# One core, attention then 64 experts: the first block's routing spread over eight pairs, and the attention's last stages placed between expert tiles

## The chip, the cores and the metric

The kernel runs on one core of a Trainium2 chip. The metric is the device time of one execution in microseconds, the median of several runs. A core has TensorE (PE in the profile; its weight loads are PEld), VectorE (DVE), ScalarE (ACT), GpSimd (POOL) and SyncE (SP, which here only issues DMAs). The engines run their own instruction streams in order and wait for each other on semaphores.

## The reference, cut to what matters

```python
x = x + attn(layernorm(x))      # x: 8 x 512 x 128, 16 heads of 64, biases; attn adds its own
                                # input and ends in a layernorm with gamma and beta
h = layernorm(x)                # 4096 tokens, 128 wide
scores = sigmoid(h @ router_w.T)            # 64 experts in 8 groups
sfc = scores + e_bias                       # choose 4 groups by the sum of their two best,
topk_idx = top8(where(group_chosen, sfc, 0))   # then 8 experts
coef = 2.5 * scores[topk_idx] / sum(scores[topk_idx])      # 0 for the other experts
g, u = h @ Wg[e], h @ Wu[e]                 # every expert, 128 -> 64
moe = sum_e (silu(g) * u * coef[:, e]) @ Wd[e]
out = x + moe + silu(h @ SWg) * (h @ SWu) @ SWd     # and a shared expert 128 -> 128
```

All experts are computed for all tokens, with coefficient 0 where an expert was not chosen. So routing is not sparse work but a chain of small operations that must be ready before a block's experts can be scaled.

## The kernel before

**Attention.** The work is 64 pairs of heads: 8 batches of 512 tokens, 8 pairs each. Each matrix factor is split into a high and a low fp16 part, and a product is three matmuls. Pair p is spread over several steps, each cut into four slots s = 0 to 3. In step p, slot by slot, TensorE computes the transposed scores of pair p (4 matmuls of 512 columns a slot, `ps_st`), the context of pair p-1 (24 short matmuls a slot, bank `ps_ctx`), the row maxima's scores for pairs p+1 and p+2 (2 matmuls a slot, `ps_max2`), in slots 0 and 1 the query and key projection of pair p+3 (`ps_proj`), in slot 2 the value projection of pair p (`ps_proj`), in slot 0 four transposes of the context of pair p-2 and in slot 3 its output product (both `ps_turn`). VectorE takes the row maxima (line 882, `row_max`), low parts (lines 908, 913, 919), the division by the softmax sum (lines 900, 902) and in slot 0 adds the output of pair p-3 to `xn` (line 891). ScalarE takes the exponentials (line 572) and high parts. GpSimd makes the low parts of the exponentials, `lo(s)` at line 437, one for each slot, and the low and high parts of one expert tile's weights over two steps (lines 449 and 453, `split_weights`). TensorE's context in step p+1 waits in slot 0 for all four `lo` of pair p.

`steps` runs p = -3 to 3 written out, p = 4 to 59 in a hardware loop of eight steps (TensorE is written out throughout), and p = 60 to 66 written out. Steps 64, 65 and 66 hold only what is left of pairs 61 to 63: the drain.

**Experts.** Then come 8 blocks of 512 tokens, each of 33 tiles: tile 0 is the shared expert, the others two experts each. A tile is gate and up (3 matmuls each), from tile 1 on one matmul that spreads the coefficients over the hidden rows (`spread`, the selector matrix that `selectors` makes on GpSimd at line 480), and down (3 matmuls). ScalarE applies silu and makes the high part of the hidden values, VectorE multiplies twice (lines 937 and 943), GpSimd makes the low part (line 471). TensorE runs four tiles ahead of `down`.

**Routing.** `route(m, r, k)` is the work of block m in numbered pieces k, the same on all engines: 1 adds the attention's bias, 2 to 6 are the post-norm (ending in line 780, `x2`), 7 to 9 the pre-norm (line 787), 8 on TensorE the transposes to `bank_c(m)`, 11 and 12 their high and low parts, then the logits, the sigmoid (14), the choice of groups (16 to 22) and experts (23 to 26), the coefficients (27, 28), their transposes (27 on TensorE), and their high and low parts (30 and 31). GpSimd has pieces 1 (constants), 2 (beta), 3 and 8 (the power -1/2, line 419) and 14. For blocks 1 to 7, piece k of block m+1 follows tile k of block m. For block 0 the pieces are placed by `block_0_at(p, s)`: pieces 1 to 16 one a slot in steps 60 to 63, and 17 to 31 three a slot from step 64. TensorE's pieces come two later (`route(0, 0, k - 2)`), and its first one waits for the last row maximum. On GpSimd a step's pieces stand behind all its `lo` and the weights. SyncE issues `load_x(0, 0)`, the input of block 0, after all its attention steps. TensorE does `gate_up(0, 0, 0)` in step 65, and the other tiles after step 66 once `spread_done` and, for tile 1, `coef_lo` are there.

The memory of the expert stage lies over buffers that the attention has finished with, in SBUF and in the eight PSUM banks.

## Time and profile before

| | |
|---|---|
| median of 3 runs | 1451.2 us (1448.94 to 1451.33) |
| the profiled execution: its own time | 1443.07 us |
| its span, first to last instruction | 1441.3 us |
| mean granted TensorE clock | 0.990 |
| TensorE matmul busy | 1362.3 us, 95% |
| VectorE busy | 1119.3 us, 78% |
| ScalarE busy | 846.5 us, 59% |
| GpSimd busy | 886.2 us, 61% |

The attention fills the first 750 us and the experts the time from 820 us on. A timeline row is start, length, engine, line, operation, shapes and count, and in brackets the idle time of the engine before it with what ended that. A merged row's length runs from the first to the last of its instructions. Idle time of an engine matters only where the engine that sets the end waits for it.

### The profile page before, as it was taken

What the parts mean: (1) busy time and instruction counts of PE and PEld (TensorE: products, weight loads), DVE (VectorE), ACT (ScalarE), POOL (GpSimd) and SP (SyncE); (2) the same over time, 40 slices, a digit from 0 to 9 for tenths busy, and PEclk for the clock granted to TensorE, in tenths of its full rate; (3) what the DMA queues carried; (4) which work ended last, traced back from release to release, by engine and by line L of the source; (5) the groups of instructions that cost most, each with busy time, mean ns of one, the idle gap of its engine ahead of it and who ended that gap; (6) DMA issues with size and microseconds to landing.
All of it is one profiled execution on the core that took longest, in us unless ns stands there. A gap on an engine that the chain in (4) does not pass through costs nothing.

```text
span 1441.3 us, 35895 instructions
## 1 busy us (share of the span) xinstructions
PE 1362.3 (95%) x12985; PEld 773.1 (54%) x12985; DVE 1119.3 (78%) x2005; ACT 846.5 (59%) x1496; POOL 886.2 (61%) x650
## 2 busy tenths in 40 slices
PE   3799999999999999999997699999999999999998
PEld 1466666666666666666665434444434444343443
DVE  6777777877787877787787688788877877787865
ACT  4566666666666666666664355554646554555554
POOL 3577767777677766767676355555555555555554
PEclk9999999999999999999999899999999999999999
DMA  6233323233333333233330000000000000000000
GB/s 179 69 73 82 78 73 78 73 78 78 85 78 82 78 73 78 73 78 74 84 79 22 8 1 8 8 8 8 1 16 0 15 0 16 0 8 8 0 8 8
DMA packets 84829, 67.42 MB, mean 47 GB/s; under 512 B 27792, under 2 KB 75216, under 8 KB 84688
## 3 DMA queue, kind: packets, MB, share of 16 engines
q1 hardware_dynamic: 84688, 65.52, 18.3%
q8 instruction: 92, 1.51, 0.4%
q14 instruction: 49, 0.40, 0.1%
HBM read 13.05 MB, written 2.10 MB: 11 GB/s over the span
## 4 chain that ended last, share of the span: by engine, by line
PE 70%; issue 13%; DVE 7%; POOL 6%; ACT 2%; SPq 2%; POOLq 0%; DVEq 0%; DMA 0%; ACTq 0%
PE bank L974 67%; POOL arena L471 4%; PE bank L1150 2%; DVE arena L937 2%; POOL arena L437 1%; DVE arena L882 1%; DVE arena L943 1%; POOL arena L419 1%; DVE arena L772 0%; ACT arena L572 0%; DVE arena L780 0%; DVE arena L787 0%; DVE arena L722 0%; ACT arena L610 0%; SPq L307 0%
## 5 line engine op out<-in xcount | busy, mean ns | idle before, releaser
L974 PE MATMUL bank<-arena 128*128 128x512 f16 (+5 forms) x12600 | 1329.1, 266 | 53.0 <-DVE arena L937 17.2
L974 PEld LDWEIGHTS bank<-arena 128*128 128x128 f16 (+3 forms) x12600 | 726.2, 98 | 622.0 <-issue 37.0
L437 POOL TENSOR_TENSOR arena<-arena 128x1024 f16<-128x1024 f32 x256 | 484.6, 1894 | 222.8 <-ACT arena L572 218.5
L471 POOL TENSOR_TENSOR arena<-arena 128x512 f16<-128x512 f32 x264 | 307.1, 1164 | 295.5 <-ACT arena L615 292.8
L882 DVE TENSOR_REDUCE arena<-bank 128x2 f32<-128x1024 f32 x256 | 312.1, 1219 | 55.5 <-PE bank L974 52.4
L572 ACT ACTIVATE arena<-bank 128x512 f32<-128x512 f32 x512 | 276.7, 596 | 89.9 <-PE bank L974 89.9
L615 ACT ACTIVATE arena<-arena 128x512 f16<-128x512 f32 x264 | 165.9, 628 | 198.0 <-DVE arena L943 197.6
L937 DVE TENSOR_TENSOR arena<-arena,bank 128x512 f32<-128x512 f32 x256 | 175.0, 684 | 88.5 <-ACT arena L610 58.5
L943 DVE TENSOR_TENSOR arena<-arena,bank 128x512 f32<-128x512 f32 x256 | 176.0, 688 | 29.3 <-DVE arena L937 5.6
L610 ACT ACTIVATE arena<-bank 128x512 f32<-128x512 f32 x264 | 155.3, 588 | 56.5 <-PE bank L974 54.8
L561 ACT ACTIVATE arena<-bank,arena 128x512 f16<-128x512 f32 x128 | 88.0, 688 | 150.4 <-PE bank L974 150.4
L913 DVE SCALAR_TENSOR_TENSOR arena<-bank,arena 128x512 f16<-128x512 f32 x128 | 95.5, 746 | 18.5 <-ACT arena L561 17.8
L919 DVE TENSOR_TENSOR arena<-bank,arena 128x512 f16<-128x512 f32 x64 | 44.3, 692 | 52.6 <-ACT arena L591 52.6
L576 ACT ACTIVATE arena<-bank 2x1024 f16<-2x1024 f32 x64 | 65.0, 1015 | 24.9 <-PE bank L974 24.8
L902 DVE TENSOR_TENSOR arena<-bank,arena 128x256 f32<-128x256 f32 x128 | 54.3, 424 | 4.4
L597 ACT ACTIVATE arena<-bank 128x512 f16<-128x512 f32 x64 | 37.7, 589 | 24.8 <-PE bank L1150 24.8
L900 DVE RECIPROCAL arena<-bank 128x4 f32<-128x4 f32 x128 | 23.4, 183 | 37.0 <-PE bank L974 35.7
L1150 PE MATMUL bank<-arena 128*128 128x128 f32 x256 | 39.5, 278 | 10.7 <-DVE arena L891 10.7
L1150 PEld LDWEIGHTS bank<-arena 128*128 128x128 f32 x256 | 32.4, 144 | 23.2 <-DVE arena L891 11.6
L891 DVE TENSOR_TENSOR arena<-bank,arena 128x512 f32 (+1 forms) x64 | 43.6, 681 | 0.9 <-PE bank L974 0.9
L908 DVE TENSOR_TENSOR arena<-bank,arena 128x512 f16<-128x512 f32 x64 | 43.6, 681 | 0.0
L591 ACT ACTIVATE arena<-bank 128x512 f16<-128x512 f32 x64 | 38.4, 600 | 1.5
(103 smaller groups left out, 417.9 us busy)
## 6 DMA issues: line engine op xcount, KB each, us to landing
arena<-arena SPq DMA_DIRECT2D x384, 128.0 KB, 2.4
arena<-in_L_attn_x SPq DMA_DIRECT2D x9, 256.0 KB, 2.9
arena<-in_L_ffn_Wg SPq DMA_DIRECT2D x32, 64.0 KB, 2.1
arena<-in_L_ffn_Wu SPq DMA_DIRECT2D x32, 64.0 KB, 2.2
arena<-in_L_ffn_Wd SPq DMA_DIRECT2D x32, 64.0 KB, 2.2
out<-arena SPq DMA_DIRECT2D x8, 256.0 KB, 2.3
arena<-in_L_attn_Wq SPq DMA_DIRECT2D x1, 512.0 KB, 3.8
arena<-in_L_attn_Wk SPq DMA_DIRECT2D x1, 512.0 KB, 5.1
```

Of the source, the lines that this page charges most:

```text
L437: pool.tensor_tensor(num_lo[:, u % 2, s, :, :], num[:, u % 2, s, :, :], num_hi[:, u % 2, s, :, :, 1], ALU.subtract).then_inc(lo_pool, 1)
L471: pool.tensor_tensor(hid_lo[:, r, :], hid[:, r, :], hid_hi[:, r, :], ALU.subtract).then_inc(hid_lo_done, 1)
L561: nc.scalar.activation(flat[:, (u + 3) % 2, (ZQH, ZKH)[which], :], ps_proj, ACT.Identity, bias=bias[:, n:n + 1]).then_inc(qk_hi, 1)
L572: nc.scalar.activation(num[:, u % 2, s, h, :], ps_st[ST_BANK[2 * s + h]], ACT.Exp).then_inc(exp_done, 1)
L610: nc.scalar.activation(silu_g[:, r % 3, :], ps_gate[r % 2], ACT.Silu).then_inc(silu_done, 1)
L615: nc.scalar.activation(hid_hi[:, r, :], hid[:, r, :], ACT.Copy).then_inc(hid_hi_done, 1)
L882: nc.vector.tensor_reduce(rmax[:, up % 2, q, :], ps_max2.rearrange("p (h k) -> p h k", h=2), AX.X, ALU.max).then_inc(max_done, 1)
L913: nc.vector.scalar_tensor_tensor(out=flat[:, (u + 3) % 2, (ZQL, ZKL)[s], :], in0=ps_proj, scalar=(bq8, bk_c)[s][:, n:n + 1], in1=flat[:, ( ...
L937: nc.vector.tensor_tensor(prod[:, i % 2, :], silu_g[:, i % 3, :], ps_up[i % 2], ALU.mult).then_inc(prod_done, 1)
L943: nc.vector.tensor_tensor(hid[:, i % 6, :], prod[:, i % 2, :], ps_coef[(k - 1) % 2], ALU.mult).then_inc(hid_done, 1)
L974: return nc.tensor.matmul(out_, lhsT, rhs, start=start, stop=stop, skip_group_check=True)
L1150: last = nc.tensor.transpose(ps_turn[:, k * P:(k + 1) * P], ctxn[:, u % 2, k, :], ident)
```

## The change

Five things change.

1. **Loop.** The hardware loop of VectorE, ScalarE, GpSimd and SyncE ends at step 52; steps 52 to 63 are written out. Steps 64 to 66 are no steps of their own any more.
2. **Routing of block 0.** It starts at step 56 (`ROUTE_0`) and each engine has a table of its own, from slot number (counted from step 56) to pieces. VectorE's pieces 1 to 12 lie in steps 56 to 58, piece 16 in step 60, 17 to 21 in step 61, 22 to 26 in step 62, 27 to 31 in step 63. GpSimd does a slot's piece right after that slot's `lo`, not behind the weights. TensorE does pieces 8 and 11 at the end of steps 58 and 59 and piece 27 at the end of step 63. `load_x(0, 0)` is issued at step 56.
3. **Drain.** The work of steps 64 and 65 on TensorE is cut into slots and placed behind `gate_up` of tiles 2, 3 and 4 and behind `down` of tiles 2 and 5. VectorE's goes before tile 0 and behind tiles 2, 3, 4, 6 and 9, ScalarE's behind tiles 2 and 5.
4. **Banks and buffers.** `bank_c(0)` is the bank of `ps_proj`, so the next projection waits for pieces 12 and 14. `ps_up` and `ps_down` change banks; `spread`, `hid` and others change places. GpSimd's piece 14 writes over projection weights and waits for the last projection, in step 60.
5. **Selectors.** GpSimd makes `spread` at the end of step 62, behind the weights, instead of after step 66. TensorE's tile 0 waits for 32 weight tiles, no longer 33, and `down` of tile 0 for the last division of the attention.

```diff
--- before.py
+++ after.py
@@ -45,7 +45,21 @@
 ST_FREE = (-1, 0, -2, 1, 2, 3, 4, 5)
-FIRST, LAST = 4, 60
+FIRST, LOOP_END = 4, 52
+ROUTE_0 = 56
...
+DVE_0 = {0: (1,), 1: (2,), 2: (3,), 3: (4,), 5: (6,), 6: (7,), 7: (8,), 9: (9,), 11: (12,), 19: (16,), 20: (17,),
+         21: (18,), 22: (19, 20), 23: (21,), 24: (22, 23), 25: (24,), 26: (25,), 27: (26,), 28: (27,), 29: (28,), 31: (31,)}
+POOL_0 = {0: (1,), 2: (2,), 3: (3,), 7: (8,), 16: (14,)}
+ACT_0 = {11: (11,), 15: (14,), 31: (30,)}
+PE_0 = {11: (8,), 15: (11,), 31: (27,)}
...
+PE_TAIL_UP = {2: ((64, 0),), 3: ((64, 1),), 4: ((64, 2), (64, 3))}
+PE_TAIL = {2: ((65, 0),), 5: ((65, 3),)}
+ACT_TAIL = {2: ((64, 0),), 5: ((65, 0),)}
+DVE_TAIL = {2: ((64, 1),), 3: ((64, 3),), 4: ((65, 0),), 6: ((65, 1),), 9: ((66, 0),)}
@@ -140,17 +154,19 @@
         top[0] = stack_at
+        spread = f16(take(E * EXPERT // 2)).rearrange("p (t n) -> p t n", t=EP)
...
         coef_split.append(f16(take(S // 2)))
-        spread = f16(take(E * EXPERT // 2)).rearrange("p (t n) -> p t n", t=EP)
+        top[0] = stack_at + 2 * 2 * 4 * S // 2
...
         prod = take(2 * S).rearrange("p (r q) -> p r q", r=2)
-        hid = take(6 * S).rearrange("p (r q) -> p r q", r=6)
+        hid = take(6 * S, num_at).rearrange("p (r q) -> p r q", r=6)
...
         ysb = take(S)
+        assert top[0] <= stack_at + 4 * 2 * 4 * S // 2 + 2 * 4 * S // 2
@@ -158,13 +174,12 @@
         ps_max2 = bank[2]
-        ps_max = ps8[4]
...
         ps_gate = [ps8[0], ps8[1]]
-        ps_up = [ps8[2], ps8[3]]
+        ps_up = [ps8[2], ps8[6]]
         ps_coef = [ps8[4], ps8[5]]
-        ps_down = ps8[6]
+        ps_down = ps8[3]
@@ -243,15 +258,16 @@
-            return ps_max if isinstance(m, int) and m == 0 else ps_turn
...
-        def block_0_at(p, s):
...
-            if not isinstance(p, int) or p < LAST:
-                return range(0)
-            slot = (p - LAST) * 4 + s
-            return range(slot + 1, slot + 2) if slot < 16 else range(slot * 3 - 31, min(slot * 3 - 28, C_PARTS))
+            return ps_proj if isinstance(m, int) and m == 0 else ps_turn
...
+        def block_0_at(parts, p, s):
...
+            return parts.get((p - ROUTE_0) * 4 + s, ()) if isinstance(p, int) and p < PAIRS else ()
...
+        def tail(run, pieces):
...
+            for p, s in pieces:
+                run(p, p % HP, p // HP, (s,))
@@ -270,10 +286,10 @@
                 run(p, p % UNROLL, p // HP)
-            with eng.Fori(0, (LAST - FIRST) // UNROLL) as i:
+            with eng.Fori(0, (LOOP_END - FIRST) // UNROLL) as i:
...
                     run(i * UNROLL + (FIRST + u), (FIRST + u) % UNROLL, i + (FIRST + u) // HP)
-            for p in range(LAST, PAIRS + 3):
+            for p in range(LOOP_END, PAIRS):
@@ -407,7 +423,7 @@
-                    pool.wait_ge(scores_t, 8 * LAST)
+                    pool.wait_ge(scores_t, 8 * ROUTE_0)
@@ -420,6 +436,8 @@
                     pool.wait_ge(sigm, m + 1)
+                    if isinstance(m, int) and m == 0:
+                        pool.wait_ge(qk_proj, 2 * PAIRS)
@@ -427,6 +445,13 @@
+            def selectors():
...
+                pool.wait_ge(scores_t, 8 * (PAIRS - 3))
+                pool.wait_ge(tri_done, 3)
+                pool.tensor_copy(spread.rearrange("p t (e n) -> p (t e) n", e=2),
+                                 twice.unsqueeze(2).broadcast_to([P, E, EXPERT])).then_inc(spread_done, 1)
@@ -453,14 +478,15 @@
-                if valid(p):
-                    for s in range(4):
+                for s in range(4):
+                    if valid(p):
                         lo(s)
+                    for k in block_0_at(POOL_0, p, s):
+                        route(0, 0, k)
...
                     split_weights()
-                for s in range(4):
-                    for k in block_0_at(p, s):
-                        route(0, 0, k)
+                if isinstance(p, int) and p == PAIRS - 2:
+                    selectors()
@@ -473,20 +499,12 @@
-            def selectors():
...
-                pool.wait_ge(scores_t, 8 * PAIRS)
-                pool.wait_ge(tri_done, 3)
-                pool.tensor_copy(spread.rearrange("p t (e n) -> p (t e) n", e=2),
-                                 twice.unsqueeze(2).broadcast_to([P, E, EXPERT])).then_inc(spread_done, 1)
...
-            selectors()
@@ -623,6 +641,8 @@
                     hid_hi_tile(n * TILES + (k - 1), (r * TILES + k - 1) % 6)
+                    if isinstance(n, int) and n == 0:
+                        tail(run, ACT_TAIL.get(k, ()))
@@ -957,12 +977,16 @@
                     tile(n, r, k)
+                    if isinstance(n, int) and n == 0:
+                        tail(run, DVE_TAIL.get(k, ()))
+                        if k == max(DVE_TAIL):
+                            dve.wait_ge(y_added, PAIRS)
...
-            dve.wait_ge(y_added, PAIRS)
+            tail(run, ((PAIRS, 0),))
@@ -1025,12 +1049,16 @@
                     if isinstance(m, int) and m == 0:
-                        pe.wait_ge(max_done, 4 * PAIRS)
+                        pe.wait_ge(v_lo_done, ROUTE_0 + 3)
+                    if isinstance(m, int) and m == 1:
+                        pe.wait_ge(y_added, PAIRS)
...
                     pe.wait_ge(tr_c_lo, m + 1)
+                    if isinstance(m, int) and m == 0:
+                        pe.wait_ge(v_lo_done, ROUTE_0 + 4)
@@ -1038,6 +1066,7 @@
                         pe.wait_ge(coef, 1)
+                        pe.wait_ge(v_lo_done, PAIRS)
@@ -1048,6 +1077,8 @@
                 t, i = n * TILES + k, r * TILES + k
+                if isinstance(n, int) and n == 0 and k == TILES - 1:
+                    pe.wait_ge(w_split, TILES)
@@ -1124,6 +1155,10 @@
                                 wait(pe, qk_lo, 2 * t)
+                            if p == ROUTE_0 + 3:
+                                pe.wait_ge(tr_c_lo, 1)
+                            if p == ROUTE_0 + 4:
+                                pe.wait_ge(sigm, 1)
@@ -1151,16 +1186,10 @@
                         rest_of_a(p, s)
-                    for k in block_0_at(p, s):
...
-                        route(0, 0, k - 2)
-                    if isinstance(p, int) and (p, s) == (PAIRS + 1, 1):
...
-                        pe.wait_ge(w_split, TILES)
-                        pe.wait_ge(exp_done, 8 * PAIRS)
-                        gate_up(0, 0, 0)
...
-            for p in range(-3, PAIRS + 3):
+                    for k in block_0_at(PE_0, p, s):
+                        route(0, 0, k)
...
+            for p in range(-3, PAIRS):
@@ -1187,13 +1216,21 @@
                     down(n, r, k)
+                    if isinstance(n, int) and n == 0:
+                        tail(run, PE_TAIL.get(k, ()))
...
-            pe.wait_ge(spread_done, 1)
-            for k in range(1, 5):
+            pe.wait_ge(w_split, TILES - 1)
+            pe.wait_ge(exp_done, 8 * PAIRS)
+            for k in range(5):
+                if k == 1:
+                    pe.wait_ge(coef_lo, 1)
+                    pe.wait_ge(spread_done, 1)
                 gate_up(0, 0, k)
+                tail(run, PE_TAIL_UP.get(k, ()))
+            pe.wait_ge(ctx_done, 2 * PAIRS)
```

The hunks left out pass `slots` to `run`, move `load_x` up in SyncE's program, put GpSimd's `selectors` at the end of its step 62, and replace the calls `block_0_at(p, s)` by `block_0_at` with the engine's table.

## Rows read from the trace of the kernel before

**Rows 1.** The windows view: us, busy (and count) by engine, clock, DMA share, GB/s.

```profile
200.00:400.00 200.00, 200.00 (x2722) 133.80 (x2721) 158.65 (x224) 132.25 (x241) 142.03 (x88) 1.00 0.33 79
...
757.10:818.00 60.90, 38.91 (x566) 28.53 (x564) 42.09 (x93) 22.45 (x39) 34.37 (x25) 0.86 0.05 12
...
769.20:776.10 6.90, 3.18 (x17) 2.01 (x18) 6.80 (x13) 0.00 (x0) 3.18 (x3) 0.56 0.01 2
803.30:813.70 10.40, 6.21 (x88) 5.99 (x88) 8.98 (x26) 0.60 (x1) 2.38 (x1) 0.54 0.01 2
817.00:820.40 3.40, 2.38 (x10) 1.86 (x11) 0.97 (x2) 0.97 (x2) 0.00 (x0) 0.62 0.00 0
802.10:817.25 15.15, 6.50 (x88) 6.01 (x88) 13.38 (x42) 0.60 (x1) 3.58 (x2) 0.66 0.01 2
820.00:850.00 30.00, 27.65 (x133) 11.86 (x132) 26.63 (x58) 15.08 (x25) 15.55 (x14) 0.98 0.03 10
```

**Rows 2.** The timeline of TensorE: start, us, count, [idle before it and its releaser].

```profile
736.33 11.34 PE L974 MATMUL bank<-arena 128*128 128x512 f16 x154
747.51 0.60 PE L1150 MATMUL bank<-arena 128*128 128x128 f32 x4
...
759.64 0.66 PE L1150 MATMUL bank<-arena 128*128 128x128 f32 x4 [1.01 <-DVE arena L891]
...
772.92 5.20 PE L974 MATMUL bank<-arena 128*128 128x512 f16 x44 [5.72 <-DVE arena L882]
...
806.68 1.11 PE L1150 MATMUL bank<-arena 128*128 128x128 f32 x4 [5.68 <-DVE arena L891]
...
818.02 1.11 PE L1150 MATMUL bank<-arena 128*128 128x128 f32 x4 [4.04 <-DVE arena L891]
...
819.78 19.25 PE L974 MATMUL bank<-arena 128*128 128x512 f16 x92
```

**Rows 3.** The timeline of VectorE, pairs 60 to 62.

```profile
749.10 0.68 DVE L757 TENSOR_TENSOR arena<-arena 128x512 f32<-128x512 f32 x1
...
752.78 0.86 DVE L761 BATCH_NORM_STATS2 arena<-arena 128x6 f32<-128x128 f32 x4
...
757.61 1.37 DVE L772 SCALAR_TENSOR_TENSOR arena<-arena 128x128 f32<-128x128 f32 x4
...
764.28 7.33 DVE L780 SCALAR_TENSOR_TENSOR arena<-arena 128x128 f32<-128x128 f32 x4
```

**Rows 4.** The timeline of GpSimd, pairs 59 to 62.

```profile
744.25 1.89 POOL L437 TENSOR_TENSOR arena<-arena 128x1024 f16<-128x1024 f32 x1 [1.09 <-ACT arena L572]
...
761.63 1.27 POOL L428 TENSOR_TENSOR arena<-arena 128x512 f32<-128x512 f32 x1 [2.46 <-DMA arena<-in_L_attn_x]
...
763.87 7.59 POOL L437 TENSOR_TENSOR arena<-arena 128x1024 f16<-128x1024 f32 x4
...
777.66 1.90 POOL L437 TENSOR_TENSOR arena<-arena 128x1024 f16<-128x1024 f32 x1
```

**Rows 5.** The source-line view, lines 780 and 787: ns min/median/max, first and last start.

```profile
L780 DVE SCALAR_TENSOR_TENSOR arena<-arena x32: 336/637/1975, 764.3 to 1304.8; 128x128 f32<-128x128 f32 x32
...
L787 DVE TENSOR_SCALAR arena<-arena x4: 334/336/338, 779.3 to 780.1; 128x128 f32<-128x128 f32 x4
```

**Rows 6.** The timeline of ScalarE, pair 63.

```profile
792.69 1.28 ACT L545 ACT_TABLE_LOAD   x1
```

**Rows 7.** The timeline of GpSimd and then VectorE, beside the selectors.

```profile
802.09 3.60 POOL L480 CAST arena<-arena 128x4096 f16<-128x4096 f32 x1
...
802.17 3.65 DVE L802 TENSOR_TENSOR arena<-arena 128x128 f32<-128x128 f32 x1 [3.64 <-POOL arena L423]
```

**Rows 8.** The page's part 5: line, form, count, busy us, mean ns, idle before.

```profile
L882 DVE TENSOR_REDUCE arena<-bank 128x2 f32<-128x1024 f32 x256 | 312.1, 1219 | 55.5 <-PE bank L974 52.4
...
L937 DVE TENSOR_TENSOR arena<-arena,bank 128x512 f32<-128x512 f32 x256 | 175.0, 684 | 88.5 <-ACT arena L610 58.5
...
L913 DVE SCALAR_TENSOR_TENSOR arena<-bank,arena 128x512 f16<-128x512 f32 x128 | 95.5, 746 | 18.5 <-ACT arena L561 17.8
```

More of the change, by code:

```diff
@@ L562, in hi @@
                                          bias=bias[:, n:n + 1]).then_inc(qk_hi, 1)
-                for s in range(4):
+                for s in slots:
                     if valid(p):
@@ L1077, in query_tile @@
                     last.then_inc(max_scores, 1)
-                for s in range(4):
+                for s in slots:
                     if valid(p):
```

31 lines of the change are left out of this document (15 added, 16 removed).

## The prediction

> **What bounds the kernel now.** I read the windows view first, to see where TensorE is not full. In the middle of the attention it is busy for all of 200 us, at a granted clock of 1.00, with VectorE at 158.65, GpSimd at 142.03 and ScalarE at 132.25 us [rows 1]. So TensorE sets the pace there, and a pair takes 747.51 - 736.33 + 0.43, about 11.6 us [rows 2]. From 757.1 to 818.0 us it is busy for only 38.91 of 60.9 us: **22.0 us idle** [rows 1]. This is the stretch with routing pieces 5 to 31 and the drain. On both sides it is nearly full: 27.65 of 30 us from 820 us on.
>
> The timeline of TensorE says who is waited for: 1.01, 5.68 and 4.04 us for VectorE's addition at line 891, and 5.72 us for the row maxima of line 882 [rows 2]. None of these operations is slow. VectorE was late because block 0's pieces stand ahead of them in its queue.
>
> The granted clock is the third reading. In three windows inside the stretch it is 0.56, 0.54 and 0.62, which is almost all at the lower level, 1.2 instead of 2.4 GHz [rows 1]. Each follows idle TensorE; the first comes with the 5.72 us wait [rows 2]. The three windows hold 3.18 + 6.21 + 2.38 = 11.8 us of busy time, and half of it, **5.9 us**, is the price of the low clock. Together 27.9 us lie in this stretch beyond TensorE's own work at full clock. All of it sits before tile 1 of the experts.
>
> **What the change takes away.** The drain's TensorE work (96 short matmuls of context, eight transposes, two output products) is not removed. It moves between matmuls of expert tiles, whose inputs are there without it. The routing no longer has to end after the last pair. If TensorE stayed full from pair 56 to the tiles, all 27.9 us would go. The sum is therefore 27.9 less the new stalls.
>
> **What VectorE can take.** Its own attention work is 158.65 / 200 x 11.6 = 9.2 us a pair, so 2.4 us are free in each of pairs 56 to 60. Steps 61 to 63 have no projections: TensorE's work falls by 6 matmuls of 512 columns, then by row maxima too, to some 10.3, 9.5 and 8.4 us (0.21 us each, from 19.25 us for 92 [rows 2]). VectorE loses two low parts of 0.746 us a step, two row maxima of 1.219 us in step 62 and four in step 63 [rows 8], and the last value part stays: 7.7, 5.3 and 2.9 us. Free in eight pairs: 5 x 2.4 + 2.6 + 4.2 + 5.5 = 24.3 us.
>
> The routing's pieces 1, 2, 4 cost 0.68, 0.86, 1.37 us [rows 3]; 7 is like 2 (0.86); 12 and 31 are of the 0.68 us form; 6 and 9 are four of 0.336 us each [rows 5], 1.3 us; 3 and 8 I estimate at half of piece 2 each. That is 9 us. Pieces 16 to 28 lie in the window 802.1 to 817.25 us, where VectorE is busy for 13.38 us [rows 1]. Off go 3.3 us of the 3.65 us operation that stood beside the selectors [rows 7], and some 2.3 us of attention operations, which leaves 7.8 us. Sum 16.8 of the 24.3 us free. So it fits over eight pairs, but not in each: pair 56 gets 3.4 us into 2.4, pair 57 2.7 into 2.4, and pair 61 (pieces 17 to 21, about 3.2 us) into 2.6.
>
> **The new stalls, step by step.**
>
> *Pair 56, pieces 1 to 4.* The kernel before did the same in pair 60, and lost 759.64 - 747.51 - 11.6 = 0.5 us [rows 2]. I take 0.5.
>
> *Pairs 57 and 58, pieces 6 to 12.* Here is the largest unknown. Before, the four operations of line 780, 0.34 us each at best, took 7.33 us [rows 3]: the four `lo` of GpSimd ran back to back beside them, 7.59 us [rows 4], and each VectorE operation ended with one of them (one lasted 1.975 us [rows 5]). GpSimd was back to back because it had stood waiting 2.46 us for the DMA of block 0's input, and its `lo` had piled up behind piece 2 [rows 4]. The change issues that DMA four steps earlier and puts the pieces between the `lo`, so the gaps of about 1.09 us between 1.89 us operations [rows 4] stay, and a gap has room for about three of line 780's operations. I expect one full block and part of a second: 1.3 to 3 us for piece 6, so 2.7 us of VectorE work becomes 4.4 at most. Row maxima must end some 0.6 to 1.3 us before TensorE's next use of the bank. Working through pairs 57 and 58 with that, I get stalls of 1.1, 0.5 and 0.5 us: 2.1. Bounds: 0.5, if all fit a gap, and 7, if all four are blocked (7.33 - 1.3 = 6.0) plus the rest.
>
> *TensorE's transposes and logits* at the end of steps 58 and 59 are work that it did before too. The next projection must wait for piece 12 in `ps_proj`: one ScalarE copy and 0.68 us, hidden by some 2.7 us of scores and context ahead of it. Piece 14 costs ScalarE two table loads of 1.28 us [rows 6] in front of pair 60's exponentials. ScalarE has 3.9 us free a pair (132.25 / 200), but scores of slot 1 need a bank that these exponentials free: I take 0.7, bounds 0 and 2.5.
>
> *GpSimd's wait for the last projection* in step 60 holds up its `lo(1)`. It ends at about the time when the late exponentials let `lo(1)` begin: nothing, at most 2, in the range of the next.
>
> *Pairs 60 and 61, pieces 16 to 21.* Thirteen small operations with both inputs in SBUF, the kind that was blocked above. Piece 16 stands at the end of step 60, beside `lo(3)` and weights: up to 1.9 us late, of which the addition at line 891 hides 1.2; I take 1.3 for both parts. In pair 61, 3.2 us go into 2.6 and some four blocks of half a `lo` and more (about 1 us) come on top: 3.0 after what the slack hides. Bounds for the two: 0.5 and 9.
>
> *Pairs 62 and 63.* The shorter TensorE steps no longer cover the chain exponential, `lo`, context: 0.35 us twice, and VectorE's few blocks: 1.2 in all. GpSimd's `selectors` (3.60 us [rows 7]) stands ahead of the `lo` of step 63, whose context is wanted only after tiles 0 to 2: hidden, bound 2. It can block pieces 27 and 28, which have 4 us until piece 27 on TensorE.
>
> *The end of step 63.* Transposes, ScalarE's copy 0.6, VectorE's low part 0.68 before tile 1. Tile 0's gate and up (6 matmuls, 1.3 us) cover most: 1.2, bounds 0.5 and 3. `down` of tile 0 waits for the last division, covered by the output product: 0.5, bounds 0 and 1.
>
> *Block 0's first ten tiles.* A tile gives VectorE two operations of 0.684 us [rows 8], TensorE ten matmuls, 2.1 us. Block 1's pieces 1 to 9 already take 7 us of VectorE there, and the drain adds 4 us to it and 5 us to TensorE. Both are about full: the 2.35 us idle of 820 to 850 us [rows 1] grows by 1.5, bounds 0 and 4.
>
> **Sum.** 0.5 + 2.1 + 0.7 + 1.3 + 3.0 + 1.2 + 1.2 + 0.5 + 1.5 = 12.0. 27.9 - 12.0 = 15.9 us less. Against the profiled execution, 1443.07 us of its own (span 1441.3), that is 1427; the median of the runs is 1451.2, so I predict 1451.2 - 15.9 = **1435 us**.
>
> **A rule beside it.** The first of line 787's four operations of piece 9 began 0.26 us before a `lo` ended (777.66 + 1.90 [rows 4], 779.30 [rows 5]) and all four lasted 334 to 338 ns: no block is seen. The Trainium skill, "SBUF — State Buffer", section "Who interferes with whom", says that not only instructions with two SBUF inputs but `tensor_scalar` too can take the port pair that VectorE shares with GpSimd, and that the second to come waits for the whole instruction. By that rule piece 9 would wait as piece 6 does, some 2 us more, and the sum would be 1437.
>
> **Rivals.**
>
> *Blocked nearly throughout, slower.* Of block 0's pieces 27 VectorE operations have both inputs in SBUF (1 + 4 + 4 + 2 + 4 + 3 + 2 + 2 + 2 + 1 + 1 + 1). If each waited for a whole `lo`, as line 780 did, that is 27 x (1.975 - 0.336) = 44 us. VectorE has 24.3 - 16.8 = 7.5 us to hide it, so 36.7 stay, and with the other terms (0.7 + 1.2 + 1.2 + 0.5 + 1.5 = 5.1) the loss is 41.8 against 27.9: 1465 us. It decides from (27.9 - 5.1 + 7.5) / 1.64, about 19 whole blocks, on. For it: GpSimd is busy for 71% of the time and the median of line 780 is 637 ns, not 336 [rows 5]. Against: a late VectorE holds TensorE, then the exponentials, then GpSimd, which opens the gaps again. 0.06.
>
> *Half is given back, in the pairs and in block 0.* VectorE is at its limit in pairs 57 and 61 and in tiles 1 to 9. If pairs 60 and 61 cost 8 rather than 4.3, pairs 57 and 58 4, and block 0 4, the sum is 20: 1443 us. For it: 13 dependent operations in step 61. 0.22.
>
> *The pieces fall into the gaps.* Pairs 57 and 58 0.5, 60 and 61 0.5, block 0 0, end of 63 and `down` 0.5, the others as above: 0.5 + 0.5 + 0.7 + 0.5 + 0.7 + 0.5 = 3.4, 1427 us. For it: pieces 17 and 18 begin at about GpSimd's gap by the present rhythm. 0.18.
>
> *No change*: only if the stall went to another place in full, such as an expert stage that keeps the whole time. Idle TensorE of 22 us is more than that stage has to give in ten tiles. 0.02.
>
> **Chances and range.** My forecast, 1430 to 1440, has 0.52. The range takes in most of the clean case and most of the half-gain case: 1426 to 1446. Faster by over 0.2% (about what a measurement of this kernel can tell from no change): 0.91; within it 0.02; slower 0.07, the blocked case and a little for what I don't see.
>
> **What would show it.** TensorE's idle time between pair 56 and tile 10 of 12 to 16 us instead of 24, no wait above 3 us; granted clock 1.00 throughout; line 780's four operations of block 0 at 1.3 to 3 us, not 7.33; TensorE's waits on VectorE lines 882 and 891 in pairs 57, 58 and 61; the first tile's matmuls right after pair 63. I am wrong if VectorE's routing operations each last near 1.9 us, if the clock falls again, if GpSimd's `lo` are late for step 61 to 63's contexts, or if block 0's tiles take more time than block 1's by several us.

## The result, and the profile after

The changed kernel takes 1428.28 us (median of 4 runs, 1426.04 to 1429.93), the kernel before 1451.26 us (1448.94 to 1451.8). The ratio of the paired runs is 0.9864, with a 95% interval of 0.9841 to 0.9886: faster by 1.4%, some 16 to 23 us. A second comparison gave 1427.1 us and 0.9849 (0.9824 to 0.9873). The forecast was 1435, in a range of 1426 to 1446: the time lies in the range, and below the 1430 to 1440 that had most of the chance.

The profiled executions differ by less, 1443.07 against 1428.47 us. In later measurements the kernel before ranged from 1441 to 1452 us and its mean granted clock from 0.992 to 0.984, with the lower clock in the longer executions; the profiled one was at the fast end. So sizes are read below from one stretch in each profile: from the four transposes of step 56 to those of piece 8 for block 1, behind tile 8. It is 148.56 us before, 131.55 after, **17.0 us less**, against 15.9 forecast. What follows is 591.7 and 591.6 us. The rest of the difference lies in front: the stretch begins at 701.07 us before and at 703.55 after. The transposes of step 4 begin at 97.0 to 98.6 us in the three profiles with the old program, and at 97.0 to 101.7 in the ten with the new one and its variants. That the change itself delays the start is neither shown nor excluded.

The timeline of TensorE after the change answers to [rows 2]. L998 is what was L974, L1185 the transposes of a step, L902 the row maxima (L882), L911 the addition (L891), L922 the division by the softmax sum (L902 before), L928 a low part (L908), L957 the first multiplication of an expert tile (L937), L1056 the transposes of piece 8 (L1030), L1071 those of piece 27 (L1042).

```profile
715.53 0.66 PE L1185 MATMUL bank<-arena 128*128 128x128 f32 x4
716.02 7.57 PE L998 MATMUL bank<-arena 128*128 128x512 f16 x107
724.91 2.94 PE L998 MATMUL bank<-arena 128*128 128x512 f16 x42 [1.32 <-DVE arena L902]
...
738.35 1.28 PE L998 MATMUL bank<-arena 128*128 128x512 f16 x14 [1.11 <-DVE arena L902]
...
754.53 0.60 PE L1185 MATMUL bank<-arena 128*128 128x128 f32 x4
...
766.09 0.66 PE L1185 MATMUL bank<-arena 128*128 128x128 f32 x4 [0.43 <-DVE arena L911]
...
777.98 0.89 PE L998 MATMUL bank<-arena 128*128 128x65 f16 x24 [2.36 <-DVE arena L922]
...
780.52 1.11 PE L1185 MATMUL bank<-arena 128*128 128x128 f32 x4 [0.81 <-DVE arena L911]
...
793.53 0.66 PE L1185 MATMUL bank<-arena 128*128 128x128 f32 x4 [1.04 <-DVE arena L911]
...
800.86 0.60 PE L1071 MATMUL bank<-arena 128*64 128x128 f32 x4
801.29 5.48 PE L998 MATMUL bank<-arena 128*128 128x512 f16 x44
...
813.64 5.14 PE L998 MATMUL bank<-arena 128*128 128x512 f16 x23 [0.53 <-DVE arena L922]
```

The waits of 5 us are gone, the longest is 2.36 us. From step 60's transposes to step 61's it is 11.55 us (754.53 to 766.09), against 12.13 with a wait of 1.01 us before, and the expert tiles begin at 801.29, in the middle of what was the drain. The windows view of the halves of the stretch, and of the one half-clock window inside it, in the columns of [rows 1]:

```profile
703.55:800.86 97.31, 88.40 (x1215) 59.02 (x1213) 83.88 (x159) 59.26 (x106) 70.55 (x46) 0.98 0.21 51
800.86:835.10 34.24, 31.67 (x252) 16.61 (x250) 30.19 (x66) 16.19 (x27) 18.93 (x17) 1.00 0.03 9
...
780.45:783.90 3.45, 3.38 (x23) 2.20 (x24) 2.08 (x5) 1.72 (x3) 0.00 (x0) 0.51 0.00 0
```

Idle in 131.55 us: 131.55 - 88.40 - 31.67 = 11.5 us. Before, between the same marks, TensorE was idle for 24 us. Of the 11.5, this is what the waits of TensorE name, from 703.5 us on:

```profile
PE bank L998 <- DVE arena L922: 3.6, 4, 2.4
PE bank L998 <- DVE arena L902: 2.9, 4, 1.3
PE bank L1185 <- DVE arena L911: 2.3, 3, 1.0
PE bank L998 <- DVE arena L957: 1.9, 2, 1.0
PE bank L998 <- DVE arena L928: 0.5, 1, 0.5
```

All of it is VectorE. No wait for `lo` (L462) or for the exponentials is left. Why VectorE is late stands in its own timeline beside GpSimd's. First VectorE's, where L800 is piece 6 (L780 before) and L807 piece 9 (L787), L846 and L847 piece 20, L874 piece 26, L879 piece 27:

```profile
720.83 2.77 DVE L800 SCALAR_TENSOR_TENSOR arena<-arena 128x128 f32<-128x128 f32 x4
...
734.48 2.68 DVE L807 TENSOR_SCALAR arena<-arena 128x128 f32<-128x128 f32 x4
...
774.18 2.14 DVE L846 TENSOR_TENSOR arena<-arena 128x256 f32<-128x256 f32 x1
776.25 1.13 DVE L847 TENSOR_TENSOR arena<-arena 128x256 f32<-128x256 f32 x1
...
793.84 2.52 DVE L879 TENSOR_SCALAR arena<-arena 128x4 f32<-128x4 f32 x1
```

And GpSimd's (L462 is `lo`, L478 weights, L453 the selectors):

```profile
720.95 1.98 POOL L462 TENSOR_TENSOR arena<-arena 128x1024 f16<-128x1024 f32 x1 [1.18 <-ACT arena L590]
...
734.60 1.97 POOL L462 TENSOR_TENSOR arena<-arena 128x1024 f16<-128x1024 f32 x1 [0.39 <-ACT arena L590]
...
774.15 1.89 POOL L462 TENSOR_TENSOR arena<-arena 128x1024 f16<-128x1024 f32 x1 [0.75 <-ACT arena L590]
776.00 1.09 POOL L478 TENSOR_TENSOR arena<-arena 128x384 f16<-128x384 f32 x1
...
792.54 3.79 POOL L453 CAST arena<-arena 128x4096 f16<-128x4096 f32 x1
```

Line 846 began 0.03 us after a `lo` and ended 0.28 us after it; line 847 ended 0.29 us after the weights (L478); line 879, on four numbers a partition, lasted until the selectors were done (792.54 + 3.79 = 796.33, and 793.84 + 2.52 = 796.36). The source-line view gives that line's other times (ns, least, median, most):

```profile
L879 DVE TENSOR_SCALAR arena<-arena x8: 169/170/2522, 793.8 to 1338.5; 128x4 f32<-128x4 f32 x8
```

### The profile page after: what moved, and what is told of

Read it like the earlier page. It is cut to its first block, busy times and chain, and to the rows that moved or that the text cites. A ratio compares the mean times of both kernels' runs of the same rounds, so it can differ in the third digit from the quotient of the medians.

```text
span 1426.7 us, 35687 instructions
## 1 busy us (share of the span) xinstructions
PE 1358.8 (95%) x12985; PEld 769.2 (54%) x12985; DVE 1119.4 (78%) x2005; ACT 847.6 (59%) x1496; POOL 888.0 (62%) x650
## 4 chain that ended last, share of the span: by engine, by line
PE 63%; issue 19%; DVE 8%; POOL 5%; SPq 2%; ACT 1%; POOLq 0%; DMA 0%; DVEq 0%; ACTq 0%
PE bank L998 61%; POOL arena L497 4%; PE bank L1185 2%; DVE arena L902 1%; DVE arena L957 1%; DVE arena L963 1%; DVE arena L792 1%; POOL arena L462 1%; DVE arena L742 0%; DVE arena L807 0%; POOL arena L435 0%; DMA arena<-arena 0%; DVE arena L922 0%; ACT arena L633 0%; SPq L323 0%
## 5 line engine op out<-in xcount | busy, mean ns | idle before, releaser
L998 PE MATMUL bank<-arena 128*128 128x512 f16 (+5 forms) x12600 | 1328.0, 265 | 52.5 <-DVE arena L957 16.9
L998 PEld LDWEIGHTS bank<-arena 128*128 128x128 f16 (+3 forms) x12600 | 724.7, 98 | 622.0 <-issue 38.0
L462 POOL TENSOR_TENSOR arena<-arena 128x1024 f16<-128x1024 f32 x256 | 484.9, 1895 | 223.8 <-ACT arena L590 220.1
L902 DVE TENSOR_REDUCE arena<-bank 128x2 f32<-128x1024 f32 x256 | 311.8, 1218 | 55.2 <-PE bank L998 51.9
L957 DVE TENSOR_TENSOR arena<-arena,bank 128x512 f32<-128x512 f32 x256 | 174.9, 683 | 88.8 <-ACT arena L628 59.0
L922 DVE TENSOR_TENSOR arena<-bank,arena 128x256 f32<-128x256 f32 x128 | 54.3, 424 | 4.4
L911 DVE TENSOR_TENSOR arena<-bank,arena 128x512 f32 (+1 forms) x64 | 43.6, 681 | 0.0
L928 DVE TENSOR_TENSOR arena<-bank,arena 128x512 f16<-128x512 f32 x64 | 43.5, 680 | 0.0
L1185 PE MATMUL bank<-arena 128*128 128x128 f32 x256 | 39.2, 276 | 2.4 <-DVE arena L911 2.3
L1185 PEld LDWEIGHTS bank<-arena 128*128 128x128 f32 x256 | 31.9, 143 | 15.5 <-DVE arena L911 4.3
```

The lines of the kernel that those rows point to most:

```text
L462: pool.tensor_tensor(num_lo[:, u % 2, s, :, :], num[:, u % 2, s, :, :], num_hi[:, u % 2, s, :, :, 1], ALU.subtract).then_inc(lo_pool, 1)
L902: nc.vector.tensor_reduce(rmax[:, up % 2, q, :], ps_max2.rearrange("p (h k) -> p h k", h=2), AX.X, ALU.max).then_inc(max_done, 1)
L957: nc.vector.tensor_tensor(prod[:, i % 2, :], silu_g[:, i % 3, :], ps_up[i % 2], ALU.mult).then_inc(prod_done, 1)
L998: return nc.tensor.matmul(out_, lhsT, rhs, start=start, stop=stop, skip_group_check=True)
L1185: last = nc.tensor.transpose(ps_turn[:, k * P:(k + 1) * P], ctxn[:, u % 2, k, :], ident)
```

## The experiments

Step lengths in what follows are the distances between two groups of a step's transposes, in one profile each. TensorE's own work is 11.6 us in steps 56 to 59, with 0.4 more for each of pieces 8 and 11. For the shorter steps the runs below show it best, where nothing waits: 10.96 us from step 60's transposes to 61's (short `lo`), 10.63 from 61's to 62's (later choice), 6.74 from 63's to piece 27's (short `lo` and split selectors); from 62's to 63's TensorE is busy for 9.1 to 9.5 us, counted at full clock. The changed kernel has, from step 56 on: 11.98, 13.65, 13.39, 11.96, 11.55, 14.43, 13.01 us, and 7.33 to piece 27's.

### The kernel before, again

Edit: none.

> The kernel before, once more, with a profile. The executions that were timed are 1448.9 to 1451.8 us, the profiled one was 1443.07, so a third of the measured gain (23 us by the medians, 14.6 us by the two profiles) has no place in the profiles yet. Theory A: the profiled execution of before was a lucky one in its first stage (up to pair 4) and in the clock of the stretch at 757 to 820 us; a new profile shows 1446 to 1452, the same 11.61 us a pair and the same 591 us after tile 8, and the surplus lies before pair 4 or in the half-clock windows. Theory B: the surplus is spread over the steady pairs or the later expert blocks; then these lengths differ by tenths of a per cent from the first profile.

Measured: 1449.11 us (1442.26 to 1451.54, 10 runs), ratio to before 1.001 (0.9989 to 1.0031). The profile was again at the fast end: span 1440.6 us, stretch 148.36 (148.56), what follows 591.6. So these two profiles agree within 0.2 us over the stretch, but both are of executions at the fast end, while the executions spread over 10 us. The changed kernel's two profiles (further below) differ by 0.5 us, all of it in how long the clock was at half. Theory B has nothing for it in the profile. Theory A is supported by the clock of the runs (0.988 to 0.992 in those under 1446 us, 0.984 to 0.986 in all above, in this measurement). My estimate from these: a mean clock lower by 0.006 over 1441 us is some 17 us more at half clock, and costs up to 9. The profiles show that the first stage can hold such time: it is 6.8 us in the first profile of the kernel before, none in the second, 3.4 and 13.7 in the two of the changed kernel. But no profile caught a long execution, so where its low clock lies stays open.

### One part alone: the input load issued early

```diff
@@ before.py, SyncE
                     wait(sp, scores_t, 8 * p)
+                    if isinstance(p, int) and p == LAST:
+                        load_x(0, 0)
...
-            sp.wait_ge(scores_t, 8 * LAST)
-            load_x(0, 0)
```

> The kernel before with one part of the change: SyncE issues block 0's input load at the start of its step 60, ahead of that step's stack and weight DMAs, instead of after them (at 758.53 us in the first profile). Theory A (mine): GpSimd no longer waits 2.46 us for it, its lo of pair 61 don't pile up to four in a row, and the four operations of line 780 take 3 to 5 us instead of 7.33; the first long stall of TensorE (5.72 us) shrinks by as much: 2 to 4 us faster than before, and no half clock at 770 us. Theory B: GpSimd is back to back there anyway, with its pieces 1 to 3 behind the weights, so the load moves nothing: within 1 us by the length of the step. Theory C: the stall shrinks there and comes back as a longer one in steps 62 to 65: step lengths fall and rise again.

Measured: 1444.98 us (10 runs), ratio 0.9983 (0.9965 to 1.0001): at most a little faster. The timeline of VectorE and of TensorE in this kernel, with the old line numbers:

```profile
765.53 3.40 DVE L780 SCALAR_TENSOR_TENSOR arena<-arena 128x128 f32<-128x128 f32 x4
...
775.50 3.84 DVE L787 TENSOR_SCALAR arena<-arena 128x128 f32<-128x128 f32 x4
```

```profile
770.24 2.94 PE L974 MATMUL bank<-arena 128*128 128x512 f16 x42 [1.80 <-DVE arena L882]
...
781.17 0.63 PE L1030 MATMUL bank<-arena 128*128 128x128 f32 x4 [3.98 <-DVE arena L882]
```

Line 780 fell from 7.33 us [rows 3] to 3.40, as I had read from the piled-up `lo`, and the step from 61's transposes to 62's from 18.32 to 13.63 us. But the next grew from 12.18 to 16.12, with a wait of 3.98 us before piece 8's transposes, and the one after was 16.55 as before. Over the stretch 0.6 us remain. The mechanism was A, the outcome C. In the old placement TensorE's piece 8 waits for the last row maximum in step 62. VectorE's piece 9 stands ahead of that maximum, and came earlier, beside a `lo`: line 787 took 3.84 us for the four operations that were 0.34 us each before [rows 5]. After the wait the clock was at half for 3.4 us, which took the rest. So the block moved from piece 6 to piece 9.

### The drain whole again

The last line of the edit stands before tile 0 on TensorE, VectorE and ScalarE.

```diff
@@ after.py
-PE_TAIL_UP = {2: ((64, 0),), 3: ((64, 1),), 4: ((64, 2), (64, 3))}
-PE_TAIL = {2: ((65, 0),), 5: ((65, 3),)}
-ACT_TAIL = {2: ((64, 0),), 5: ((65, 0),)}
-DVE_TAIL = {2: ((64, 1),), 3: ((64, 3),), 4: ((65, 0),), 6: ((65, 1),), 9: ((66, 0),)}
+PE_TAIL_UP = {}
+PE_TAIL = {}
+ACT_TAIL = {}
+DRAIN = tuple((p, s) for p in (64, 65) for s in range(4)) + ((66, 0),)
+DVE_TAIL = {9: ()}
...
+            tail(run, DRAIN)
```

> The changed kernel with only the drain's placement undone: steps 64, 65 and 66 run whole, after pair 63 and before tile 0. Theory A (mine): its chain of division, transposes, copy, low part, output product and addition, twice, with nothing between, leaves TensorE idle for 4 to 6 us and costs some at half clock: 4 to 8 us slower than the changed kernel, 1433 to 1437, so that two thirds or more of the gain come from the routing's spread. Theory B: the drain is where the 22 us of idle TensorE were; then it is 12 us or more slower, 1440 and above. Theory C: it hides the chain of piece 27 to 31 and costs next to nothing, within 2 us.

Measured: 1433.9 us (5 runs), 5.6 us more than the changed kernel's 1428.28; the stretch 140.12 against 131.55, 8.6 us more. The timeline of TensorE shows the chain; the clock is granted at half for 3.4 us from 805.6 and again from 812.4 us:

```profile
803.29 0.35 PE L1000 MATMUL bank<-arena 128*128 128x65 f16 x6 [1.50 <-POOL arena L463]
...
805.64 3.80 PE L1000 MATMUL bank<-arena 128*128 128x65 f16 x60 [0.81 <-DVE arena L924]
810.22 0.65 PE L1187 MATMUL bank<-arena 128*128 128x128 f32 x4 [0.78 <-DVE arena L913]
812.29 18.05 PE L1000 MATMUL bank<-arena 128*128 128x128 f16 x84 [1.42 <-DVE arena L930]
```

Theory A for the time. Of the 8.6 us, 8.1 lie behind piece 27's transposes (42.30 against 34.24 us), and 0.5 in a longer half-clock window before them, as the changed kernel itself has in its second profile. So taking the placement of the drain away costs 8.1 us of the 17.0, and what stays is 8.9: about half and half rather than one third and two. That holds for this order only. The drain alone, with the routing in its old place, was not run, nor with tile 0's `gate_up` inside the drain, where the kernel before had it.

### Is it the port? Short lo

```diff
@@ after.py, GpSimd
+                    n = 64 if isinstance(p, int) and p >= ROUTE_0 else S
-                    pool.tensor_tensor(num_lo[:, u % 2, s, :, :], num[:, u % 2, s, :, :],
-                                       num_hi[:, u % 2, s, :, :, 1], ALU.subtract).then_inc(lo_pool, 1)
+                    pool.tensor_tensor(num_lo[:, u % 2, s, :, 0:n], num[:, u % 2, s, :, 0:n],
+                                       num_hi[:, u % 2, s, :, 0:n, 1], ALU.subtract).then_inc(lo_pool, 1)
```

> The changed kernel, with GpSimd's low parts of the exponentials (lo) of pairs 56 to 63 computed for 64 of 512 columns only, so the output of these pairs is not the reference's; the instructions, their order and their waits stay. Theory A (port): VectorE's operations with two SBUF inputs, and the tensor_scalar of lines 807 and 874, are long because they wait for a whole lo of 1.89 us. With short lo the four of line 800 take 1.2 us instead of 2.77, the four of line 807 1.2 instead of 2.68, lines 846 and 847 0.42 each instead of 2.14 and 1.13; the stall of 2.36 us in pair 61 and the half-clock stretch after it go, in all 5 to 8 us faster than the changed kernel, about 1421. Theory B (queue): VectorE is late because of the number of its operations and their waits; their lengths fall, but the pairs lose 0 to 2 us only. Theory C: the lo themselves are late for the context; then pairs 62 and 63 gain and 57 and 58 don't.

Measured: 1425.34 us (4 runs), 2.9 less than the changed kernel where A gave 5 to 8; the stretch 128.97, 2.6 less. The operations did what theory A says in steps 57 and 58:

```profile
722.79 1.27 DVE L801 SCALAR_TENSOR_TENSOR arena<-arena 128x128 f32<-128x128 f32 x4
...
734.95 1.19 DVE L808 TENSOR_SCALAR arena<-arena 128x128 f32<-128x128 f32 x4
```

2.77 became 1.27 and 2.68 became 1.19 us, and the steps 12.16 and 12.11 us (13.65 and 13.39). Step 61 fell by less, to 12.87 (14.43): its line 848, which is 847 in the changed kernel, still lasted 1.13 us beside the weights. Steps 62 and 63 got longer: 13.82, and 14.58 from step 63's transposes to step 64's (13.01 and 13.08). The reason is the other long operation of GpSimd, which now came earlier. VectorE, GpSimd and TensorE in turn:

```profile
786.74 3.42 DVE L875 TENSOR_SCALAR arena<-arena 128x256 f32<-128x256 f32 x1
```

```profile
786.42 3.60 POOL L453 CAST arena<-arena 128x4096 f16<-128x4096 f32 x1
```

```profile
791.35 1.11 PE L1186 MATMUL bank<-arena 128*128 128x128 f32 x4 [3.58 <-DVE arena L912]
```

A `tensor_scalar` of piece 26, 0.28 us of work, stood behind the selectors for 3.42 us, the addition behind it, and TensorE's transposes behind that. So the size of A was missed while its mechanism was met twice.

### Short lo and selectors in eight parts

As before, and:

```diff
@@ GpSimd, end of slot s in steps 61 and 62, instead of selectors() after the weights of step 62
+                    if isinstance(p, int) and p in (PAIRS - 3, PAIRS - 2):
+                        selectors(4 * (p - PAIRS + 3) + s)
```

Each call makes the selectors of 8 of the 64 experts.

> The changed kernel with GpSimd's lo of pairs 56 to 63 computed for 64 of 512 columns only, as in the run with the short lo (the output of these pairs is not the reference's), and with the selectors (3.79 us in one operation, beside which line 875 lasted 3.42 us and the addition of line 912 came 3.58 us late in that run) cut into eight parts, one behind each lo of steps 61 and 62. Theory A (port): what steps 61 to 63 still lose (12.87, 13.82 and 14.58 us long where 10.3, 9.0 and 8.6 us are TensorE's own work) is the wait of tensor_scalar and two-input operations for the selectors and the half clock that follows; both go, no operation of the choice lasts over 1 us, and the three steps together fall by 6 us or more, 1417 to 1420. Theory B: these short steps are bound by the chain of exponentials, division, transposes and low parts between ScalarE and VectorE; then they fall by 2 us at most, 1423 or more.

Measured: 1420.11 us (4 runs), the stretch 123.62 us, 7.9 less than the changed kernel. Steps 61 and 62 are 12.64 and 10.75 us, and step 63 to 64 12.49, together 5.4 less than with short `lo` alone, where A gave 6 or more (4.6 less than in the changed kernel). No operation of the choice lasts over 0.82 us. No granted clock below 1.00 after the first stage and before the end. What TensorE still waits for:

```profile
771.96 0.90 PE L1001 MATMUL bank<-arena 128*128 128x65 f16 x24 [0.56 <-DVE arena L925]
...
774.57 0.66 PE L1188 MATMUL bank<-arena 128*128 128x128 f32 x4 [0.87 <-DVE arena L914]
...
779.38 4.30 PE L1001 MATMUL bank<-arena 128*2 128x128 f16 x60 [0.53 <-DVE arena L931]
```

So of the changed kernel's loss in this stretch 7.9 us go when GpSimd's operations are short: VectorE operations that waited for them, and the half clock behind that. TensorE is still idle for 6.0 us, with VectorE named in each wait. The division and the additions that it waits for stand right behind pieces of the choice, so I read the rest as VectorE's queue, which A had left out; no run separates it from theory B's chain.

### The choice later, the selectors split, both, and the norm too

Four variants compute all of the reference. The first has another table for VectorE:

```diff
@@ after.py
-         21: (18,), 22: (19, 20), 23: (21,), 24: (22, 23), 25: (24,), 26: (25,), 27: (26,), 28: (27,), 29: (28,), 31: (31,)}
+         21: (18, 19), 24: (20,), 25: (21,), 26: (22, 23), 27: (24,), 28: (25, 26), 29: (27,), 30: (28,), 31: (31,)}
```

> The changed kernel with another table for VectorE: pieces 18 and 19 in slot 21, 20 in 24, 21 in 25, 22 and 23 in 26, 24 in 27, 25 and 26 in 28, 27 in 29, 28 in 30. Step 61 then has pieces 17 to 19 (1.8 us) instead of 17 to 21 (3.4 us) where 2.6 us are free, and steps 62 and 63 have 3.4 and 3.6 where 4.2 and 5.5 are. Theory A: the stall of pair 61 (4.1 us by the step's length) falls to 1 or less, the half-clock stretch goes, pairs 62 and 63 lose at most 1 more: 3 to 5 us faster than the changed kernel, 1423 to 1425. Theory B: the same two-input operations are blocked by lo wherever they stand; same time within 1.5 us, the stall moves to pair 62. Theory C: piece 28 now comes late for TensorE's piece 27, and the end of step 63 loses 2 us or more.

Measured: 1425.65 us (4 runs). That is 2.6 less than the changed kernel, where A gave 3 to 5. The step from 61's transposes to 62's is 10.63 us, TensorE's own work, 3.8 less. But the next two are 12.86 and 15.42 (13.01 and 13.08). In its timeline of VectorE, line 857 is a `tensor_scalar` of 32 numbers a partition:

```profile
784.68 1.90 DVE L857 TENSOR_SCALAR arena<-arena 128x32 f32<-128x32 f32 x1
...
790.91 2.00 DVE L875 TENSOR_TENSOR arena<-arena 128x256 f32<-128x256 f32 x1
```

A in step 61, B in 62 and 63: the stretch is 129.97 us, 1.6 less. The end of step 63 lost 2.3 us (9.66 instead of 7.33 to piece 27's transposes), as C has it, but without a wait: the clock is at half there for 6.8 us.

The second has the changed kernel's table and the selectors in eight parts, with the edit shown above:

> The changed kernel with the selectors alone cut into eight parts, one behind each lo of steps 61 and 62, in place of one operation of 3.79 us at the end of step 62. Theory A (port): in the changed kernel lines 874 and 879 (0.93 and 2.52 us) waited for it; they fall to 0.3, the step from pair 61's transposes to pair 62's to the end shortens by 1 to 2 us: 1426 to 1427.5. Theory B: nothing on TensorE's path waited for it, since piece 27 has four us: same time within 1 us. Theory C: the parts make lo later for the contexts of pairs 61 and 62: slower by 1 to 3 us.

Measured: 1428.2 us (4 runs), the stretch 132.26 us against 131.55. Theory B for the time. From step 63's transposes to piece 27's it got 0.6 us shorter, steps 61 and 62 0.9 and 0.4 longer. In step 61 VectorE's piece 21 (lines 854 and 855 in this run) took 1.30 and 0.71 us, and TensorE waited 1.53 us for the addition behind it. The 0.4 in step 62 goes with a half-clock window of 6.8 instead of 3.4 us, which the changed kernel has too in its second profile. No wait for `lo` shows, so C's mechanism was not met.

The third has both:

> Both together: VectorE's pieces 18 to 28 later, as in the run with the later table (1425.65), and the selectors in eight parts. Theory A (port): there the stall had moved to steps 62 and 63 (12.86 and 15.42 us), where line 857 lasted 1.90, 874 0.88 and 875 2.00 us beside lo and selectors; without the long operation 2 to 4 us go: 1422 to 1424. Theory B: they are blocked by lo whatever the selectors do: within 1 us of 1425.65.

Measured: 1423.54 us (4 runs), 2.1 less than with the later table alone, at the lower edge of what A gave; the stretch 128.94 us, 1.0 less, which is B's. The timelines are on B's side. The two operations of piece 26 met three `lo` in a row in place of the selectors, and the division that TensorE's context waits for stood behind them. VectorE, GpSimd and TensorE in turn:

```profile
789.36 2.04 DVE L876 TENSOR_SCALAR arena<-arena 128x256 f32<-128x256 f32 x1
791.44 2.00 DVE L877 TENSOR_TENSOR arena<-arena 128x256 f32<-128x256 f32 x1
```

```profile
789.36 5.83 POOL L464 TENSOR_TENSOR arena<-arena 128x1024 f16<-128x1024 f32 x3
```

```profile
794.04 3.85 PE L1000 MATMUL bank<-arena 128*128 128x65 f16 x76 [2.29 <-DVE arena L924]
```

Again, beside the changed kernel:

> The later table with the selectors in eight parts again, beside the changed kernel: 128.9 us for the stretch against 131.6, 2.6 us faster by the profiles, 1422 to 1427 by the runs. If the two medians differ by less than 1 us here, the 4.7 us of the first comparison were the spread of the executions.

> The changed kernel once more, beside the run of the later table with split selectors on the same chip. Its stretch from step 56 to block 1's piece 8 was 131.55 us; I expect it within 0.3 us of that, the runs 1426 to 1430, and the spread between executions in the first 100 us and in the clock.

Measured: 1425.17 against 1427.1 us (4 runs each), with ratios to the kernel before of 0.9843 (0.9818 to 0.9867) and 0.9849 (0.9824 to 0.9873). The stretch was 128.87 against 132.04 us, the latter with a half-clock window of 6.8 instead of 3.4 us at 780 us, and so 0.5 off the 131.55 from which I had expected 0.3 at most. So this version is faster in both comparisons, by 4.7 and 1.9 us of the medians and 2.6 and 3.2 of the stretch. The profiles' difference is clear of their own spread (0.1 and 0.5 us); the runs' intervals overlap.

The fourth spreads the norm's pieces as well:

```diff
-DVE_0 = {0: (1,), 1: (2,), 2: (3,), 3: (4,), 5: (6,), 6: (7,), 7: (8,), 9: (9,), 11: (12,), ...
+DVE_0 = {0: (1,), 1: (2,), 2: (3,), 4: (4,), 6: (6,), 7: (7,), 8: (8,), 10: (9,), 11: (12,), ...
-POOL_0 = {0: (1,), 2: (2,), 3: (3,), 7: (8,), 16: (14,)}
+POOL_0 = {0: (1,), 2: (2,), 3: (3,), 8: (8,), 16: (14,)}
```

> As the run with the later table and split selectors, and the norm's pieces spread as well: VectorE's pieces 4, 6, 7, 8, 9 in slots 4, 6, 7, 8, 10 instead of 3, 5, 6, 7, 9, and GpSimd's piece 8 in slot 8. Theory A: the stalls of steps 57 and 58 (13.65 and 13.39 us, against 11.61 and 12.06) come from four-operation pieces beside lo and from 3.4 and 2.7 us of pieces where 2.4 are free; spread over more slots they fall by 1 to 2 us together: 1421 to 1423. Theory B: each of the four-operation pieces meets a lo in any slot, since the gaps are 1.09 us: no change against the run before it. Theory C: piece 9 one slot later delays the transposes of piece 8 on TensorE, which wait at the end of step 58: 1 to 2 us slower.

Measured: 1429.9 us (4 runs), and the stretch 132.76, 3.8 more than without it. Step 57 to 58 is 17.26 us. In its timeline both four-operation pieces met a `lo`:

```profile
717.77 2.98 DVE L794 SCALAR_TENSOR_TENSOR arena<-arena 128x128 f32<-128x128 f32 x4
...
725.95 3.42 DVE L802 SCALAR_TENSOR_TENSOR arena<-arena 128x128 f32<-128x128 f32 x4
```

```profile
730.10 3.55 PE L1000 MATMUL bank<-arena 128*128 128x65 f16 x29 [1.94 <-DVE arena L924]
...
744.41 0.66 PE L1058 MATMUL bank<-arena 128*128 128x128 f32 x4 [1.76 <-DVE arena L809]
```

Piece 4 took 2.98 us in slot 4 where it had been 1.17 in slot 3, and TensorE's piece 8 waited 1.76 us for piece 9. Piece 9 there took 2.87 us (2.68). B and C, and beyond them: which slot has a gap decides, and free time counted over a pair says nothing of it.

## Why the prediction was right

The sum was 27.9 taken away less 12.0 of new stalls, 15.9 us; the stretch gave 17.0. Term by term:

- **What was there to take.** 22.0 us idle stands. The low clock was under-counted: my windows sat 0.8 us early. In the trace it is granted at half from 770.04 to 776.87, 804.20 to 814.40 and 817.80 to 821.25 us, and TensorE is busy there for 3.95 + 6.50 + 3.23 = 13.7 us, so half of it is 6.8, not 5.9. That makes 28.8 us.
- **Pair 56**, 0.5: 0.37.
- **Pairs 57 and 58**, 2.1: 2.0 + 1.4 = 3.4, over the transposes' 0.4. Piece 6 was right (1.3 to 3 us, it took 2.77, one `lo` and the rest in the gap). Piece 9 I took at 1.3 us, and it took 2.68. That it would wait as piece 6 does was the rule that I had set beside the row: the Trainium skill, "SBUF — State Buffer", section "Who interferes with whom", counts `tensor_scalar` among those that can take the shared port pair. The trace agrees with it: line 807 ran long beside a `lo` (one of its four 1.92 us, the others 0.33), line 874 beside another (0.93), line 879 beside the selectors (2.52), and with a short `lo` the four of line 807 were 1.19 us. What the runs show is that these operations end behind GpSimd's and are short when GpSimd's is; that a shared port is the reason is the page's account. By the rule the term would have been 4.1, off by 0.7 and not by 1.3. My row showed only that an operation begun in the last 0.26 us of a `lo` isn't visibly longer.
- **The table loads of piece 14**, 0.7: nothing. Step 59 to 60 is at TensorE's own 11.96 us, and no wait behind them is for ScalarE.
- **Pieces 16 to 21**, 4.3: 0.6 + 3.8 = 4.4. Step 60 to 61 is 11.55 us against 10.96: the two operations of piece 16 were 0.66 and 0.58 us (0.28 and 0.29 with short `lo`), and the addition behind them came 0.43 us late. In step 61 (14.43 against 10.63) lines 846 and 847 alone were 2.14 and 1.13 us, and the 2.36 us wait follows them.
- **Steps 62 and 63**, 1.2: 3.5 + 0.6 = 4.1, one of the two terms that were far off. From step 62's transposes to 63's TensorE is idle for 1.8 us, and the half clock after step 61's waits takes 1.7; 0.6 more comes until piece 27 (7.3 us from step 63's transposes, 6.7 in the run with short `lo` and split selectors). I had counted the chain exponential, `lo`, context and few blocks. The context never waited for `lo`; the runs show VectorE's choice operations waiting for `lo` and selectors, and its queue.
- **End of step 63, `down`, block 0's tiles**, 3.2: 0.2, the other. From piece 27's transposes to block 1's piece 8 it is 34.24 us, against 849.62 - 818.93 = 30.7 before. The drain brought 4.5 us of TensorE's work into it (in a full step 24 context matmuls take 0.73, the transposes 0.43, an output product 0.66 us; four, two and one of them came in), and before it lost 1.2 at half clock (up to 821.24), so 29.7 stand against 29.5. Idle time says the same, 2.6 us against 2.35. `down`'s wait of 0.53 was the forecast 0.5.

New stalls so come to 0.4 + 3.4 + 4.4 + 4.1 + 0.2 = 12.5, and 28.8 - 12.5 = 16.3 against 17.0 measured. The windows view gives the whole without my counts: TensorE is idle for 24.4 us of the stretch before and 11.5 after, loses 6.8 and 1.7 to the half clock, and is busy for 1.0 us longer otherwise, 12.9 + 5.1 - 1.0 = 17.0.

So the mechanism was right, idle time and low clock taken away less VectorE's lateness beside GpSimd, and the closeness of 15.9 to 17.0 was in part luck: the errors of single terms, +2.9 for steps 62 and 63, +1.3 for pairs 57 and 58, -3.0 for the end and -0.7 for the table loads, nearly cancelled. Two slips in the working change nothing: pieces 16 to 21 are fifteen operations (thirteen are those of 17 to 21), and the sum of the clean case has 0.7 for steps 62 and 63 where the list has 1.2.

Of the signs that I named, no wait over 3 us, piece 6 under 3 us and waits on VectorE's additions and maxima came true, though the division (L922) has more of the waiting, 3.6 us, than either. Idle time is 11.5 us, just under the 12 to 16. A clock of 1.00 throughout did not come true: 3.4 us at half remain, and a clock that falls again stood among the signs of being wrong. That the medians moved by 23 us and not 17 is the kernel before, whose executions sit some us above its profiled one.

Of the rivals, the blocked case is refuted in its size: in the changed kernel four of the operations lasted as long as a whole `lo` or longer (one of line 800, one of line 807, lines 846 and 879), not 19. The half-gain case had the right place in steps 57 and 61 and the wrong one in block 0. The clean case is what the run with short `lo` and split selectors shows, 8 us below.

## What to carry to other kernels

A stall whose named culprit is a short operation belongs to what stands ahead of it in its queue, and there to what that operation waited for: here 0.34 us operations took 1.9 us beside another engine's, and no view lists this as a wait, since it counts as busy time. When such work is spread into a full pipeline, count free time by the gap in which an operation lands, not by the stage; moving one input load alone moved the stall by one step and gained almost nothing, and adding slots cost 3.8 us. Drain work with long chains between engines is best put between independent matmuls: there it brought one wait of 0.53 us, and run whole in front of them it cost 8.1 us.

## What the runs showed of the hardware that I had not expected

A `tensor_scalar` on 4 float32 numbers a partition, 0.17 us alone, lasted 2.52 us beside a GpSimd cast of 4096 elements a partition. Two table loads on ScalarE (1.28 us each) in front of a pair's exponentials brought no wait of TensorE. And executions of one unchanged kernel spread over 10 us, with the mean granted clock between 0.984 and 0.992; two profiles of it, both of fast executions, agree within 0.2 us over the stretch.
